# Diff attention: row sums of three key tiles added on GpSimd, factors loaded singly

## The reference, cut to what matters

```
qkv = x @ W_attn                     # q1, k1, q2, k2: 16 heads of 16; v: 16 heads of 32
lam = exp(lq1 . lk1) - exp(lq2 . lk2) + LAMBDA_INIT
attn1 = einsum('bthd,bshd->bhts', q1, k1) * scale
attn2 = einsum('bthd,bshd->bhts', q2, k2) * scale
score = softmax(attn1 - lam * attn2, axis=-1)
out = einsum('bhts,bshd->bthd', score, v)
return ((1.0 - LAMBDA_INIT) * out.reshape(B, T, E)) @ W_proj
```

## Time and profile before

| | |
|---|---|
| median of 3 runs | 2285.66 us (2281.95 to 2292.4) |
| the profiled execution | 2283.14 us, span 2281.3 us |
| TensorE | 2109.4 us busy, 92% of the span |
| VectorE | 1745.9 us, 77% |
| ScalarE | 954.7 us, 42% |
| GpSimd | 1063.7 us, 47% |
| mean granted clock of TensorE | 0.976 |
| diff attention (inner part) | about 1700 to 2200 us of the span |

### The profile page before, as it was taken

The page is one execution under the profiler, slowest core; times in us unless marked ns, Lnnn a source line. Parts: engine busy times, 40 slices in busy tenths (PEclk is TensorE's granted clock), DMA queues, the critical chain, the costliest instruction groups (busy, mean ns, idle before and its releaser), DMA issues. The chain is left out here.

```text
span 2281.3 us, 25381 instructions
## 1 busy us (share of the span) xinstructions
PE 2109.4 (92%) x7542; PEld 1134.9 (50%) x7542; DVE 1745.9 (77%) x2990; ACT 954.7 (42%) x1825; POOL 1063.7 (47%) x810
## 2 busy tenths in 40 slices
PE   6999999999999998998899899999979999999989
PEld 3455455545545553443555646556454544545344
DVE  3888888878887878787798988988846556464775
ACT  2443333324423433664664646547324323242331
POOL 3552443333433441322899899999942101110143
PEclk9999999999999999999999999999989999999999
DMA  7000000000000003445853636535165334242221
GB/s 278 19 24 19 19 19 24 19 19 24 19 19 24 19 15 104 169 168 189 317 180 109 211 127 212 180 102 198 56 200 151 112 83 122 72 119 71 75 92 65
DMA packets 100089, 230.63 MB, mean 101 GB/s; under 512 B 16510, under 2 KB 33792, under 8 KB 97812
## 3 DMA queue, kind: packets, MB, share of 16 engines
q1 hardware_dynamic: 86216, 181.61, 24.2%
q10 hardware_dynamic: 13260, 47.73, 5.9%
q0 software_dynamic: 512, 0.13, 0.0%
HBM read 157.84 MB, written 45.22 MB: 89 GB/s over the span
## 5 line engine op out<-in xcount | busy, mean ns | idle before, releaser
L1617 POOL TENSOR_TENSOR s_state<-s_b_rows,s_delta_u 128x1024 f32<-128x1024 f32 x128 | 303.4, 2383 | 36.5 <-DMA s_b_rows<-scan_bc 34.1
L928 POOL TENSOR_SCALAR a_prob<-a_prob,a_rsum 128x256 f32<-128x256 f32 x256 | 143.5, 580 | 376.3 <-DVE a_rsum L801 376.2
L1660 DVE TENSOR_TENSOR_SCAN s_state<-s_decay,s_state 128x512 f32<-128x512 f32 x256 | 304.9, 1211 | 15.6 <-ACT s_decay L1603 13.2
L1777 PE MATMUL c_bank<-c_xn_parts,c_w_parts 128*128 128x512 f32 (+1 forms) x1056 | 270.3, 406 | 2.4 <-DVE c_xn_parts L1855 1.4
L1603 ACT ACTIVATE s_decay<-s_delta,s_a 128x512 f32<-128x512 f32 x256 | 173.5, 689 | 222.3 <-DVE s_state L1660 219.0
L453 DVE TENSOR_SCALAR f_picks<-f_mask,f_lut_xor,f_lut 128x260 int32<-128x260 int32 x512 | 228.8, 519 | 7.6 <-DVE f_mask L444 0.8
L1777 PEld LDWEIGHTS c_bank<-c_xn_parts,c_w_parts 128*128 128x128 f32 (+1 forms) x1056 | 196.4, 187 | 63.0 <-issue 13.9
L600 PE MATMUL a_bank<-a_xn_t,a_wq_then_context 128*128 128x512 f32 x512 | 224.3, 592 | 0.0
L661 PE MATMUL a_bank<-a_wo,a_out_t 128*128 128x512 f32 x512 | 222.3, 592 | 0.0
L2342 ACT ACTIVATE d_prob_t<-d_score 128x512 f32<-128x512 f32 x256 | 139.0, 596 | 178.8 <-PE d_score L2193 178.2
L463 DVE COPY_PREDICATED f_picks<-f_mask,f_picks 128x260 int32<-128x260 int32 x448 | 193.7, 492 | 21.1
(11 more groups left out here) (242 smaller groups left out, 3732.9 us busy)
## 6 DMA issues: line engine op xcount, KB each, us to landing
s_b_rows<-scan_bc SPq DMA_DIRECT2D x64, 512.0 KB, 3.7
c_w_parts<-ffn_weights_hi ACTq DMA_DIRECT2D x39, 512.0 KB, 3.7
c_w_parts<-ffn_weights_lo ACTq DMA_DIRECT2D x39, 512.0 KB, 4.9
d_unit<-diff_parts SPq DMA_DIRECT2D x26, 512.0 KB, 3.6
f_idx<-in_idx SPq DMA_DIRECT2D x64, 130.0 KB, 2.2
ffn_weights<-f_picks SPq DMA_DIRECT2D x64, 130.0 KB, 1.8
d_qs<-d_hi SPq DMA_DIRECT2D x128, 64.0 KB, 2.0
r_xn<-in_factors SPq DMA_DIRECT2D x16, 512.0 KB, 3.6
```

The costliest lines, as they stand in the source:

```text
L1617: pool.tensor_tensor(self.state[:, s], row.broadcast_to([P, 2, T]), self.delta_u[:, h % 2], ALU.mult) \
L1660: dve.tensor_tensor_scan(self.state[:, s, e, :], self.decay[u % 2][:], self.state[:, s, e, :], 0.0, ALU.mult, ALU.add).then_inc(self.scann ...
L1777: mm = nc.tensor.matmul(banks[b][0:width[o], :], w_parts[:, n % SLOTS, w, at:at + width[o]], xn_parts[:, x_, k, :], start=((k, w, x_) == t ...
```

## The change

In every group but the last of all (`kept`), GpSimd adds the exponentials of key tiles 0 and 1, and then of tile 2, into two kept tiles `sums` of 128x1024 (two heads each), which take the place of the factors in `rows_kept`: four additions of 128x1024 a group (`keep_sums`). TensorE multiplies ones with the kept sum once, at tile 2, and with tile 3 itself: two products with ones (of four heads each) where there were four. `prob_used` now comes with the product with values. The new semaphore `summed` counts the additions; ScalarE waits for it before it writes over a tile, TensorE before it reads the sum. The factors are loaded one at a time into a tile of their own, `factor`: the first as before, the second between q's copies and k's weights on SP (`load_factor`), and GpSimd adds the first before `keep_sums` and the second after `store_maxima`. `mask_bf` is now held only as long as the first layer's attention, which makes room for `factor`; the places of tiles in memory shift by it.

```diff
-    factor = rows_kept[:].rearrange("p (s r) e -> p s r e", s=2)
-    factor_in = core.sems("d_factor_in", 2)
+    factor = sb("d_factor", [P, D], F32)
+    factor_in = core.sem("d_factor_in")
+    sums = [rows_kept[:, 2 * half:2 * half + 2, :] for half in range(2)]
+    summed = core.sem("d_summed")
...
+            def load_factor(i, g, r):
+                if r == 0:
+                    sp.wait_ge(max_in, (i * GROUPS + g) * 16 + 16)
+                sp.wait_ge(factor_added, (i * GROUPS + g) * PER_PASS + r + 1)
+                sp.dma_start(factor[:], dram["factors"][bass.ds(i * PER_PASS + r, 1), g * P:(g + 1) * P, :]
+                             .rearrange("r p e -> (r p) e")).then_inc(factor_in, 16)
...
                             stack(sp, ring, i, kind, pg)
+                            if kind == "q":
+                                load_factor(i, g, 1)
+                    else:
+                        load_factor(i, g, 1)
                     if g < GROUPS - 1:
-                        load_factors(i, g + 1)
+                        load_factor(i, g + 1, 0)
                     elif more:
-                        load_factors(i + 1, 0)
+                        load_factor(i + 1, 0, 0)
...
+            def weigh(n, g, st, kept):
...
+                    mm = nc.tensor.matmul(acc[j * VD:(j + 1) * VD, :], v[:, st, h * VD:(h + 1) * VD],
+                                          prob_t[:, st % 2, j, :], start=(st == 0), stop=(st == TT - 1))
+                if kept and st < TT - 1:
+                    mm.then_inc(prob_used, 1)
+
+            def add_up(st, first_one):
+                for j in range(HG):
+                    mm = nc.tensor.matmul(acc_sum[j * VD:(j + 1) * VD, :], consts.ones[:, 0:VD],
+                                          prob_t[:, st % 2, j, :], start=first_one, stop=(st == TT - 1))
+                mm.then_inc(prob_used if st < TT - 1 else acc_full, 1)
+
+            def add_up_kept(n):
+                pe.wait_ge(summed, n * 4 + 6)
+                for j in range(HG):
+                    nc.tensor.matmul(acc_sum[j * VD:(j + 1) * VD, :], consts.ones[:, 0:VD],
+                                     sums[j // 2][:, j % 2, :], start=True, stop=False)
...
+                    kept = more or g + 1 < GROUPS
...
-                        weigh(n, g, st, 0)
+                        weigh(n, g, st, kept)
                         if st < TT - 1:
                             columns(n, g, st + 1, 1)
                         if st < 2 and rows_on:
                             rows(ring, i, rg, *ROWS_AT[2 * st + 1])
-                        weigh(n, g, st, 1)
+                        if not kept:
+                            add_up(st, st == 0)
+                        elif st == TT - 2:
+                            add_up_kept(n)
+                        elif st == TT - 1:
+                            add_up(st, False)
...
+                if st == 0:
+                    act.wait_ge(summed, n * 4 + half + 1)
+                elif st == 2 and kept:
+                    act.wait_ge(summed, n * 4 + half + 3)
...
+            def keep_sums(n, st, half):
+                for s in range(2):
+                    pool.wait_ge(exp_done[s], n * FILLS + st * 2 + half + 1 + 1)
+                if st == 1:
+                    pool.wait_ge(acc_full, n + 1)
+                    left = prob_t[:, 0, 2 * half:2 * half + 2, :]
+                else:
+                    pool.wait_ge(summed, n * 4 + half + 3)
+                    left = sums[half]
+                nc.gpsimd.tensor_tensor(sums[half], left, prob_t[:, st % 2, 2 * half:2 * half + 2, :], ALU.add) \
+                    .then_inc(summed, 1)
...
                 for g in range(GROUPS):
-                    add_factors(i, g)
+                    n = i * GROUPS + g
+                    add_factor(i, g, 0)
                     if more or g + 1 < GROUPS:
+                        for st in (1, 2):
+                            for half in range(2):
+                                keep_sums(n, st, half)
                         store_maxima(ring, i, (g + 1) % GROUPS)
+                    add_factor(i, g, 1)
```

More of the change, by code:

```diff
@@ L131, in __init__ @@
         self.ident_bf = sb("ident_bf", [P, P], BF16)
-        self.mask_bf = sb("mask_bf", [P, 2, 2 * P], BF16)
+        self.mask_bf = None
         self.minus_half = sb("minus_half", [P, TT], F32)
@@ L2117, in _ @@
             sp.wait_ge(w_stored, 16 * 2 * GROUPS)
-            load_factors(0, 0)
+            load_factor(0, 0, 0)
             passes(sp, one_pass)
@@ L2194, in columns @@
                                      qs[0:3 * E2 + 1, h, :], start=True, stop=True).then_inc(score_full[s], 1)
[L2196 to L2202, removed]
+            def weigh(n, g, st, kept):
+                if st == 0:
+                    pe.wait_ge(acc_free, n + 1)
+                for s in range(2):
+                    pe.wait_ge(exp_done[s], n * FILLS + st * 2 + 2 + 1)
                 for j in range(HG):
                     h = g * HG + j
[L2205 to L2209, removed]
+                    mm = nc.tensor.matmul(acc[j * VD:(j + 1) * VD, :], v[:, st, h * VD:(h + 1) * VD],
[12 more added lines that the diff above has]
+                                     sums[j // 2][:, j % 2, :], start=True, stop=False)
             def one_pass(i, more):
@@ L2329, in high, with exponentials @@
                                      scale=1.0 if m else coef[:]).then_inc(hi_done, 1)
-            def exponentials(n, st, half):
+            def exponentials(n, st, half, kept=True):
                 if half == 0:
@@ L2351, in one_pass @@
                         if st > 0:
-                            exponentials(n, st + 1, 0)
+                            exponentials(n, st + 1, 0, kept)
                         if st < 2 and proj_on:
@@ L2355, in one_pass @@
                         if st == 0:
-                            exponentials(n, 1, 0)
-                        exponentials(n, st + 1, 1)
+                            exponentials(n, 1, 0, kept)
+                        exponentials(n, st + 1, 1, kept)
                     if g == 1 and more:
@@ L2567, in split_pieces @@
                         .then_inc(w_split, 1)
+            pool.sem_inc(summed, 2)
             split_pieces(0, 2 * KD)
@@ L2837, in program @@
         ahead = {name: Ahead(sb, name) for name in ("ffn_first", "diff_first", "mix_first") + GATES_AHEAD}
-        with ExitStack() as stage:
-            sb, psum = keeper(stage)
-            stage_setup(core, sb, dram, x, consts)
-        core.clear()
         with ExitStack() as both:
             wide = keeper(both)[0]("a_wq_then_context", [P, KD * HEADS * HD], F32)
-            with ExitStack() as held:
-                stage_window_attention(core, *keeper(held), dram, x, consts, scratch, wide)
-            core.clear()
+            with ExitStack() as masked:
+                consts.mask_bf = keeper(masked)[0]("mask_bf", [P, 2, 2 * P], BF16)
+                with ExitStack() as held:
+                    stage_setup(core, keeper(held)[0], dram, x, consts)
+                core.clear()
+                with ExitStack() as held:
+                    stage_window_attention(core, *keeper(held), dram, x, consts, scratch, wide)
+                core.clear()
             with ExitStack() as held:
```

14 lines of the change are left out of this document (7 added, 7 removed).

## The result

The changed kernel takes 2294.02 us in the median of 20 runs (2289.48 to 2300.47), the kernel before 2291.07 us in 20 runs beside them (2281.52 to 2296.83). The ratio is 1.0022, with a 95% interval of 1.0011 to 1.0032. So the change costs about 5 us, in place of the 18.5 us forecast: the sign and the range held, the size did not. The profiled execution took 2291.35 us.

A forecast was written before the change was run, and what follows sets the result against it. VectorE's maxima were taken to set the pace at two places, with TensorE just behind. From 2285.7 us, exceptions -2.6, SP +0.4 and the clock +20.7 gave +18.5: 2304.2 us, range 2280 to 2318 (8 in 10).

The forecast's parts named there:

- What bounds the kernel: Diff attention, 1700 to 2190 us: VectorE's maxima set the pace at two places, TensorE within 0.2 to 0.3 us.
- The rival that TensorE is the bound: Maxima start earlier by an overlooked route, so all 29.7 us come off: 2256.0 us, chance 0.04.
- Worth 0 at tile 0: Ahead of the second projection: the removed 0.99 us becomes wait, 0.18 to 1.17 us, and gains 0.
- Worth 0 at tile 1: Ahead of the transpose of the maxima: the wait grows from 0.32 to 1.31 us, so the removal gains 0.
- Exceptions, -2.6 us: Last group but one of pass 3, -0.99 us; normalised rows in group 1 of passes 1 and 2, -0.8 each.
- What is added, cost 0 on GpSimd and ScalarE: GpSimd's four additions, 9.5 us a group, end in time; ScalarE's new waits are met before its scores: cost 0.
- SP's factor load: 15 more loads in mid-group, about 0.4 us each, fit a 0.45 us gap; +0.4 us for the first group.
- The rival of a late GpSimd: Additions of 4.8 us delay storing the maxima and the next group's scores, 13 us: 2297 us, chance 0.05.
- The clock term, +20.7 us: TensorE's clock falls behind the thinned stretch at the transpose: 9 falls in 15 groups, 2.3 us each; bounds 0 and 34.5.
- -2.2 for the rest: All terms except the clock: exceptions of -2.6 us and +0.4 us for SP's load in the first group.
- the stretch at 2145 us: 2145 to 2155 us, short products without long wait, clock 0.66, 3.4 us missing; among three of five thin stretches with falls.
- the rival of the clock that stays up: Added waits are too short or far apart for the clock to fall: 2283.5 us, not slower, chance 0.27.

The follow-up runs named there:

- the values first: The changed kernel with key tile 2's products with values moved ahead of the transpose of the maxima: 2266.84 us, 0.9905 of the kernel before.
- tile 1 filled: The changed kernel with four useless products of ones and v at key tile 1, ahead of the transpose: 2283.63 us, 0.9975 of the kernel before.
- both filled: The changed kernel with four useless products of ones and v at each removed set's place, key tiles 0 and 1: 2284.23 us, 0.9985 of the kernel before.
- filling the one ahead of the projection: The changed kernel with four useless products of ones and v at key tile 0 only: 2295.02 us, 1.0023 of the kernel before.
- the move alone: The kernel before, all four sets with ones kept, with key tile 2's products with values moved ahead of the transpose: 0.9977 of the kernel before.
- VectorE's maxima halved: The kernel before with row maxima over 256 of the 512 keys: 0.9935 of the kernel before.

## Why the prediction was right or wrong

**What bounds the kernel: right.** Taking 22 us of work from an engine that is 95% busy in the stage gained nothing. The maxima kept their place against TensorE, with the same 0.92 and 0.57 us ahead of them. The rival that TensorE is the bound (2256.0) is excluded by every run of the change as it stands.

**Worth 0 at tile 0: right to 0.2 us, with the wait in another place.** I forecast a wait of 1.17 us ahead of the projection. It shows 0.19, and the other microsecond lies inside the four row products, 2.08 for 1.09. The nine maxima ran in 5.47 in place of 5.65: the removed set had held back one of them by 0.18 us, which I had read as a run without a gap.

**Worth 0 at tile 1: right.** The wait was forecast as 1.31 us and is 1.51, because a set costs its neighbours a little as well: from the five row products to the end of the scores behind them it was 1937.90 - 1934.57 = 3.33 us with it and is 2.15 without, 1.18 less and not 0.99.

**Exceptions, -2.6 us: right in kind, too small.** The normalised rows take 1.45 us in place of 2.43, 0.98 gained in each of two groups, where I took 0.8. In the last group but one of pass 3 the wait of 1.07 us in front of the maxima is gone, and fourteen of them run on. And about 0.2 us come in each of the other twelve groups, which I had at nothing: from one transpose to the next it is 1809.66 - 1784.77 = 24.89 us in the kernel before and 1818.79 - 1794.10 = 24.69 with the change. An estimate from these rows is 2 x 0.98 + 1.07 + 12 x 0.2 = 5.4 us. With the idle stretch filled again at tile 1, which leaves all of this in place, the ratio is 0.9975, so that all gains together come to 5.7 us, between 2 and 9 by the interval. The clock is no part of it: over its 12 executions it is 0.972, where the kernel before has 0.973.

**What is added, cost 0 on GpSimd and ScalarE: right in the cost, wrong in one reason.** An addition takes 2380 ns, the forecast 2383, and the issue of the maxima still waits for VectorE. But I had ScalarE's new waits met before its scores are there, and 14 of them are not: ScalarE stands for 1.42 us in most groups. It costs nothing because TensorE needs that key tile only later. SP's factor load showed no cost in the change. With the values first it stands in front of k's copies, for which TensorE then waits; no run moved it, so a cost there is not shown. The rival of a late GpSimd (2297) is out: the kernels with tile 1 filled and with both filled have its work and are faster than before.

**The clock term, +20.7 us: the step that failed, in size.** The mechanism was the right one, and at the place named: filling the stretch ahead of the transpose removes the cost, filling the one ahead of the projection removes none. The term was 9 falls behind transposes at 2.3 us, each "lost in full". Behind the transposes there were 4 slow sets of 15 in one execution and 7 in the other, so the count was too high there, while further falls stood elsewhere, such as the one in the second projection at 1986.76. Over all executions the change has 17 us more of missing clock, which is ten falls of 1.7 us; in number the 9 were near, in part by luck. What was wrong is the price of a fall. Beside the transpose at 1945.29, here is one of the same execution that kept its clock:

```profile
1868.41 0.27 PE L2189 MATMUL d_bank<-ident,d_mx 128*16 128x128 f32 x1 [1.51 <-DVE d_mx L2455]
...
1873.23 0.74 PE L2199 MATMUL d_score<-d_qs,d_ks 97*128 97x512 f32 x2
```

From the transpose to the first step behind the last sum it is 1873.23 - 1868.41 = 4.82 us here, and 1951.42 - 1945.29 = 6.13 us where the clock fell: 1.31 us, where the clock that was missing is 7 x 0.24 = 1.7: not lost in full. The 4 to 7 falls behind transposes make 5 to 9 us at 1.3. The executions of the change give a price as well: among the 20, one with 1 us more of missing clock took 0.58 us longer, which for 17 us is 10 us, an estimate. Measured, the term is the difference between the change and the change with tile 1 filled, 1.0022 - 0.9975 = 0.0047, **10.8 us in place of 20.7**, give or take 4 by the two intervals. With -5.7 in place of -2.2 for the rest, that is the +5 us found; as both terms are taken from the same run, this sum closes of itself. The 2.3 us had been an average in which the stretch at 2145 us stood for 3.4 against 1.7 of the others; and that stretch, which has no long wait, was in the count of 3 of 5 because its clock had caught my eye.

The Trainium skill (TensorE: Matmul & The Clock Gate, "HAM oscillation — how this bites in real kernels") ties the fall to idle gaps longer than those that this change makes. The runs disagree: 1.51 us ahead of a transpose, between short products, is followed by the low clock in 4 to 7 of 15 groups, and with tile 1 filled, where that wait is 0.32, in none. The same page of the Trainium skill, section "A second HAM failure mode: psum-queue depth-cycling", has the right kind of stretch. It names no size, and the upper end that I hung on it, 34.5 us, is three times what was measured.

**The chances.** 0.60 for slower by over 0.5% was too much, and 0.35 for within 0.5% too little. I had set the border between the forecast and the rival of the clock that stays up at 6 falls of 2.3, 13.8 us. The kernel landed below it, at 10.8, by more falls at a lower price: its time is nearer that rival's, but by a mechanism that is not the rival's. Of the signs that I named, the clock over 1700 to 2190 came to 0.96 in one execution and to the 0.94 forecast in the other, and slow sums stood in 4 and 7 of 15 groups and not in more than half. The absolute time also came closer than the change did, by luck: my base of 2285.66 was a median of three, and 20 executions have 2291.07.

**What stays open.** Why the clock falls behind one transpose and not behind the next, after what looks like the same 1.51 us, is not settled, and neither is why falls also come elsewhere in the changed stage. That kernels of the same text differ by 10 us in one stage between two executions is seen, not explained further than by their clock.

## What to carry to other kernels

Work that stands next to a short wait is not on the critical path, however busy its engine looks. Before taking it away, look for the work that can move into its place: here the removal alone cost 5 us, the move alone gained 5, and the two together gained 22. Read the mean duration of a group against its undisturbed one too, because an engine that waits between the instructions of one group shows a longer busy time and no wait. And where TensorE is left with short products and idle time in one stretch, the clock is a cost of its own: filling it with products that nobody needs was faster than leaving it empty.

## What the runs showed that I had not expected

- Useless products made the changed kernel 10.8 us faster (1.0022 to 0.9975). Filling one place was no worse than filling both (0.9985), and the stage then ran at a clock of 1.00.
- Four row products paced by their banks stand in the timeline as 2.08 us of TensorE, 0.99 us more than they need, and five as 1.68 where 1.41 is enough. The busy share of 95% in the earlier trace rows had such time in it: with VectorE's maxima halved, the kernel before gained 14.9 us from waits that add up to half of that.
- The same program's stage took 468.20 and 477.81 us in two profiled executions, at clocks of 0.97 and 0.95. The clock on record for all executions, 0.973 before and 0.965 after, shows what two such profiles cannot.
